# The last batch's tail beside the first shared steps, its first norm inside attention's first iteration, and the router in the second unit of each iteration

## The reference

```
h = layernorm(x) * (1 + ca) + sa
q, k = rms_norm(h) @ W + b;  v = h @ W_v + b          # 16 heads of 16
q, k = rotary(q), rotary(k)
weights = sigmoid(q k^T / 4);  weights /= sum(weights)
x = x + ga * ((weights @ v) @ W_o + b)
h = layernorm(x) * (1 + cb) + sb
shared = (silu(h @ sg) * (h @ su)) @ sd
probs = sigmoid(h @ router_w + routing_bias);  w = top-2 of 8, normalised
routed = sum_e w_e * (silu(h @ wg_e) * (h @ wu_e)) @ wd_e
x = x + gb * (shared + routed)
```

## Time and profile before

| | |
|---|---|
| median of 3 runs | 1613.15 us (1610.79 to 1613.45) |
| profiled execution | 1611.74 us, span 1610.0 us |
| PE busy | 1464.9 us (91%) |
| DVE busy | 1140.0 us (71%) |
| ACT busy | 929.5 us (58%) |
| POOL busy | 417.0 us (26%) |
| mean granted clock of PE | 0.953 |

### The profile page before, as it was taken

The page is one execution under the profiler, slowest core; times in us unless marked ns, Lnnn a source line. Parts: engine busy times, 40 slices in busy tenths (PEclk is TensorE's granted clock), DMA queues, the critical chain, the costliest instruction groups (busy, mean ns, idle before and its releaser), DMA issues. The chain is left out here.

```text
span 1610.0 us, 29263 instructions
## 1 busy us (share of the span) xinstructions
PE 1464.9 (91%) x10406; PEld 1172.9 (73%) x10406; DVE 1140.0 (71%) x2334; ACT 929.5 (58%) x1172; POOL 417.0 (26%) x413
## 2 busy tenths in 40 slices
PE   6899999868999977899999999866999999999998
PEld 4788888757888875355545544446889999999987
DVE  4677777568878875665786686455568787877768
ACT  2566665434555534776776676743347777777752
POOL 1122322330001012232153344223213333333320
PEclk9899999989999987999999999987999999999999
DMA  7000000210000000120000000005038888888864
GB/s 275 1 1 0 0 0 0 79 42 1 0 0 0 0 27 1 70 91 1 2 29 12 22 25 22 18 18 195 28 103 231 231 234 235 231 236 232 235 157 157
DMA packets 65455, 130.51 MB, mean 81 GB/s; under 512 B 8249, under 2 KB 38754, under 8 KB 64866
## 3 DMA queue, kind: packets, MB, share of 16 engines
q1 hardware_dynamic: 51074, 110.37, 22.1%
q0 software_dynamic: 14304, 19.15, 5.7%
HBM read 97.50 MB, written 32.00 MB: 80 GB/s over the span
## 5 line engine op out<-in xcount | busy, mean ns | idle before, releaser
L1822 ACT ACTIVATE at_wide<-at_sc_ps 128x2048 f32<-128x2048 f32 x128 | 240.6, 1879 | 117.3 <-PE at_sc_ps L1658 116.1
L2276 POOL DMA_INDIRECT sums<-e_y,e_row_ids x78 | 121.6, 1559 | 247.8 <-ACT e_y L2431 235.9
L52 PE MATMUL e_gate_ps<-e_h_parts,e_w 128*128 128x256 f32 (+1 forms) x1128 | 176.9, 304 | 7.0 <-DVE e_w L2485 3.4
L2485 DVE TENSOR_TENSOR e_w<-e_raw,e_w 128x1024 fp32r<-128x1024 f32 x123 | 147.1, 1222 | 42.7 <-ACT e_w L2384 42.7
L52 PE MATMUL e_up_ps<-e_h_parts,e_w 128*128 128x256 f32 (+1 forms) x1128 | 175.0, 302 | 0.0
L52 PEld LDWEIGHTS e_gate_ps<-e_h_parts,e_w 128*128 128x128 f32 x1128 | 155.3, 193 | 14.7 <-DVE e_w L2485 3.5
L52 PEld LDWEIGHTS e_up_ps<-e_h_parts,e_w 128*128 128x128 f32 x1128 | 155.2, 193 | 7.9
L1672 PE MATMUL at_o_ps<-at_wide,at_v_ones 128*32 128x512 f32 x1024 | 142.5, 630 | 0.0
L2341 PE MATMUL e_down_ps<-e_w,e_hidden 128*128 128x256 f32 x936 | 127.9, 286 | 1.0 <-DVE e_hidden L2534 1.0
L2384 ACT ACTIVATE e_w<-e_raw 128x1024 fp32r<-128x1024 f32 x123 | 125.3, 1048 | 6.1 <-DMA e_raw<-in_experts 6.1
L1658 PE MATMUL at_sc_ps<-at_qT,at_kT 32*128 32x512 f32 x1024 | 96.3, 450 | 28.9 <-ACT at_wide L1822 26.9
(11 more groups left out here) (351 smaller groups left out, 2735.2 us busy)
## 6 DMA issues: line engine op xcount, KB each, us to landing
e_raw<-in_experts SPq DMA_DIRECT2D x123, 512.0 KB
e_rows_in<-slots SPq DMA_DIRECT2D x39, 272.0 KB
sums<-shared SPq DMA_DIRECT2D x17, 256.0 KB
x<-in_L_attn_x SPq DMA_DIRECT2D x8, 512.0 KB, 9.4
gate<-gates SPq DMA_DIRECT2D x4, 1024.0 KB
slots<-shared SPq DMA_DIRECT2D x15, 272.0 KB
out<-x SPq DMA_DIRECT2D x7, 512.0 KB, 3.1
e_sums<-sums SPq DMA_DIRECT2D x4, 512.0 KB, 4.4
```

The costliest lines, as they stand in the source:

```text
L52: last = pe.matmul(out, left(i), right(j), start=n == 0, stop=n == len(steps) - 1)
L1822: nc.scalar.activation(wide[:, u % 2, :], sc_ps[:].rearrange("p n s -> p (n s)"), ACT.Sigmoid, scale=float(HD) ** -0.5).then_inc(sig_done, 1)
L2276: pool.indirect_dma_start(c.sums_dram[:, :], bass.IndirectOffsetOnAxis(ap=row_ids[:, j % 2, t:t + 1], axis=0), y[:, j % 2, t, :], None, co ...
L2485: nc.vector.tensor_tensor(w[:, buf, REST, q], raw[:, q], w[:, buf, HEAD, q].bitcast(F32), ALU.subtract).then_inc(w_split, 1)
```

## The change

The tail of batch 7 moves past the barrier. The weights of the shared expert are loaded while attention still runs, into a buffer `early` that also holds attention's `qk`, `turned` and `rotated`, once the last rotation is done. In the last part DVE adds the gated rows to x ahead of step 0, and takes statistics, places and normalises beside step 0; PE turns the batch behind step 0; ACT modulates it; router, first half of make_rows, probabilities and `choose` stand beside step 1, the token count behind it and the list of tiles beside step 2. Steps 0 and 1 are written out, with `beside` functions after product i. PE waits for each third of the weights apart.

The first norm of batch 7 moves from the head of attention into iteration 0 (statistics, norm, transposes in unit 14, modulation of half k=0 after sigmoid 15) and iteration 1 (half k=1 after sigmoid 0, the squares on PE after attend 0, their mean on DVE, the power on POOL). DVE keeps the first quarter of batch 0 before it rotates the last.

In iterations 2 to 7 rank and router move from unit 0 to unit 1, behind attend, into bank 1 of `a_ps`; the halves of make_rows go to the ends of units 0 and 3, values 2 and 3 from unit 1 to unit 2 (in all iterations), ACT's copies of rows to units 1 and 4 and its probabilities to unit 3. Waits follow the banks. On POOL the second cosine product and `bias_x` come earlier, two scatters a unit later.

```diff
+        self.early_loaded = [self.sem(f"early_loaded_{q}") for q in range(3)]
...
-        qk, turned, rotated = sb("qk", [P, 2, 2 * D]), sb("turned", [P, 2, 2 * D]), sb("rotated", [P, 2, 2 * D])
+        qk, turned, rotated = (c.early[:, n].rearrange("p (u n) -> p u n", u=2) for n in range(3))
...
+                sp.wait_ge(rot_done, NT * B)
+                for q in range(3):
+                    sp.dma_start(c.early[:, q], a["experts"][0][:, q]).then_inc(c.early_loaded[q], 16)
...
                     if coming:
                         times_cos(b + 1, 0)
+                        times_cos(b + 1, 1)
                     if b >= 3:
                         ds.tag(pool, b - 3)
                     scatter(b, 0)
-                    if coming:
-                        times_cos(b + 1, 1)
-                    scatter(b, 1, 5)
                     if past:
                         bias_x(b - 1)
+                    scatter(b, 1, 6)
                     scatter(b, 2, 7)
+                    if b == 1:
+                        pool.wait_ge(last_kept, 1)
+                        nc.gpsimd.tensor_tensor(c.inv_rms[:, B - 1], c.mean_square[:, B - 1], c.neg_half[:, 0:NT], ALU.pow
+                                                ).then_inc(last_kept, 1)
                     if past:
                         norm.invert(pool, b - 1)
-                    scatter(b, 3, 8)
+                    else:
+                        norm_last.invert(pool, 0)
+                    scatter(b, 3, 9)
                     scatter(b, 4, 10)
...
-                pool.wait_ge(last_kept, 1)
-                nc.gpsimd.tensor_tensor(c.inv_rms[:, B - 1], c.mean_square[:, B - 1], c.neg_half[:, 0:NT], ALU.pow
-                                        ).then_inc(last_kept, 1)
...
-                norm.invert(pool, B - 1)
...
+                        if b == 2 and t in (0, 2):
+                            pe.wait_ge(last_kept, 1)
                         if t == 0:
                             pe.wait_ge(h_split, b + 1)
                             if b >= 3:
-                                pe.wait_ge(logits_kept, b - 2)
-                            if b >= 4:
-                                pe.wait_ge(ds.placed, b - 3)
+                                pe.wait_ge(next_done, KC * (b - 3) + 1)
+                        if t == 2 and b >= 3:
+                            pe.wait_ge(logits_kept, b - 2)
                         if t == 2 and b >= 4:
-                            pe.wait_ge(ds.rows_kept, 2 * (b - 4) + 1)
+                            pe.wait_ge(ds.placed, b - 3)
...
+                    if b >= 2 and b < B - 1:
+                        pe.wait_ge(ds.rows_kept, 2 * (b - 1))
+                    if not coming:
+                        pe.wait_ge(logits_kept, b)
+                        pe.wait_ge(ds.placed, b - 1)
...
+                def last_by_feature():
+                    pe.wait_ge(qT_kept, NT * 2)
+                    pe.wait_ge(kT_kept, NT * 2)
+                    pe.wait_ge(last_rows_done, 1)
+                    transposes(nc.tensor, c, a_ps, rows_by_token(B - 1)).then_inc(last_turned, 1)
+
+                def sum_last_squares():
+                    pe.wait_ge(last_h_done, KC)
+                    pe.wait_ge(tables_set, 1)
+                    for t in range(NT):
+                        for k in range(KC):
+                            last = nc.tensor.matmul(a_ps[:, 1, t:t + 1], last_squares[:, k, t * P:(t + 1) * P], ones[:],
+                                                    start=k == 0, stop=k == KC - 1)
+                    last.then_inc(last_squares_done, 1)
...
-                        if u == 0 and b >= 2:
-                            pe.wait_ge(next_done, b - 1)
-                            if b >= 3:
-                                ds.rank(pe, b - 3, ranks)
-                            route(b - 2)
-                            if b >= 3:
-                                ds.make_rows(pe, b - 3, 0, a_ps[:, 1, :])
                         attend(b, par, u)
                         if u % NT == 1 and u > NT:
                             quad_by_token(b, u // NT - 1)
+                        if u == 14 and not past:
+                            last_by_feature()
+                        if u == 0 and b == 1:
+                            sum_last_squares()
...
+                                if b >= 3:
+                                    pe.wait_ge(ds.rows_kept, 2 * (b - 3) + 1)
+                                    ds.rank(pe, b - 3, ranks(1))
+                                if b >= 2:
+                                    route(b - 2, 1)
...
-                        if b >= 3 and u == 2:
-                            if coming:
-                                pe.wait_ge(v_kept, 2 * (b + 1) + 2)
-                            pe.wait_ge(ds.rows_kept, 2 * (b - 3) + 1)
-                            ds.make_rows(pe, b - 3, 1, a_ps[:, 1, :])
...
                                 values(b + 1, 0, 1)
-                            elif u == 1:
+                            elif u == 2:
                                 values(b + 1, 2, 3)
-                            elif u in (2, 3):
+                            if u in (2, 3):
...
+                        if b >= 3 and u == 0:
+                            pe.wait_ge(next_done, KC * (b - 1))
+                            ds.make_rows(pe, b - 3, 0, a_ps[:, 1, :])
+                        if b >= 3 and u == 3:
+                            if coming:
+                                pe.wait_ge(qk_scaled, NT * (b + 1) + 1)
+                            ds.make_rows(pe, b - 3, 1, a_ps[:, 0, :])
...
-                pe.wait_ge(last_rows_done, 1)
-                transposes(nc.tensor, c, o_ps, xn_last).then_inc(last_turned, 1)
...
-                ds.rank(pe, B - 2, sc_ps[:, 3, 0:NT * E])
-                next_by_feature(B - 1, False)
-                route(B - 1)
...
+                def modulate_last(k):
+                    act.wait_ge(last_turned, 1)
+                    shift, scale = c.mod[:, 1, SA, k, B - 1:B], c.mod[:, 1, CA, k, B - 1:B]
+                    nc.scalar.activation(c.hT[:, k, B - 1, :], a_ps[:, k, :], ACT.Identity, bias=shift, scale=scale)
+                    nc.scalar.activation(last_squares[:, k, :], a_ps[:, k, :], ACT.Square, bias=shift,
+                                         scale=scale).then_inc(last_h_done, 1)
...
+                        if u == 15 and not past:
+                            modulate_last(0)
+                        if u == 0 and b == 1:
+                            modulate_last(1)
...
-                        if b >= 3 and u in (1, 3):
-                            ds.keep_rows(act, b - 3, u // 2, a_ps[:, 1, :])
-                        if b >= 2 and u == 2:
+                        if b >= 3 and u == 1:
+                            ds.keep_rows(act, b - 3, 0, a_ps[:, 1, :])
+                        if b >= 3 and u == 4:
+                            ds.keep_rows(act, b - 3, 1, a_ps[:, 0, :])
+                        if b >= 2 and u == 3:
...
-                modulate(B - 1)
-                act.wait_ge(logits_kept, B)
-                ds.probabilities(act, B - 1)
...
                 def iteration(b, par, past, coming, h_after=True):
                     n, p = b + 1, b - 1
+                    if b == 1:
+                        dve.wait_ge(last_squares_done, 1)
+                        nc.vector.tensor_scalar(c.mean_square[:, B - 1], a_ps[:, 1, 0:NT], 1.0 / D, RMS_EPS, ALU.mult,
+                                                ALU.add).then_inc(last_kept, 1)
                     if past:
                         keep_quad(p, QUADS - 1)
-                    if b >= 2:
-                        keep_logits(b - 2)
-                    if b >= 3:
-                        ds.place_tokens(dve, b - 3, ranks)
                     if coming:
                         keep_values(n, 0)
                     if past:
                         divide_quad(p, QUADS - 1)
+                    if b >= 2:
+                        keep_logits(b - 2, 1)
+                    if b >= 3:
+                        ds.place_tokens(dve, b - 3, ranks(1))
...
+                        norm_last.gather(lambda t: c.x[:, B - 1, t, :])
+                        norm_last.aggregate(dve, 0)
...
+                        norm_last.apply(dve, 0, rows_by_token(B - 1), lambda t: c.x[:, B - 1, t, :], last_rows_done)
...
-                rotate(0, 3)
                 dve.wait_ge(strips_set, 2)
                 keep_by_feature(0, 0)
+                add_turned(0, 2)
+                rotate(0, 3)
...
-                update_x(B - 1)
-                moments(B - 1)
-                normalise(B - 1)
-                ds.place_tokens(dve, B - 2, sc_ps[:, 3, 0:NT * E])
-                keep_logits(B - 1)
...
+        raw = c.early
...
-                for q in range(PARTS):
-                    load_weights(0, q, a["experts"][0])
```

(93 more changed lines are left out.)

135 lines of the change are left out of this document (59 added, 76 removed).

## The result

The changed kernel takes 1591.87 us (median of 4 runs, 1589.79 to 1593.44) against 1611.97 for the kernel before (1609.64 to 1613.45): a ratio of 0.9878, with a 95% interval of 0.9864 to 0.9892, 20.1 us less. The prediction was 1595.3, with a range of 1589 to 1604. The profiled executions stand at 1593.44 and 1611.74, so the traces explain 18.3 us.

The account below looks back on a forecast made before the run. PE was taken to bound the shared and expert steps, and sigmoid, PE's extra work and clock falls attention's iterations. Terms -10.8 + 3.3 - 10.3 = -17.8 us against the profiled 1611.74, plus 1.4 to the median, gave 1595.3 us, range 1589 to 1604.

Parts of the forecast that it names:

- Part 1, the seam: Between attention and shared steps: 19.6 us gained, less 4.0 work, 4.0 waits and 0.8 clock, so -10.8 us.
- Work brought back, 4.0: Shared steps 0 to 2 on PE: rank 0.47, router 1.79, eight transposes 1.0, token count 0.7; together 4.0 us.
- The stall, 3.7: Step 1: PE waits 3.7 us before its last down products, behind table loads and choose; the tile list costs 0.3 in step 2.
- The clock behind the stall, 0.8: After step 1's stall: a clock fall would cost 1.6 us; half was taken, 0.8.
- rival 6: Step 1's two table switches also cost 1.38 us of drain each, 2.8 us more: 1598.1 us; chance 0.05.
- Part 2, the first norm: Attention's head and iterations 0 and 1: head -2.2 us, iteration costs and half a clock fall, net +3.3 us, a loss.
- Part 3, the router: Iterations 2 to 7: PE's work the same, gain from the clock no longer falling; two falls in six assumed, -10.3 us.
- 1 (all six fall): Iterations 2 to 7: the clock still falls briefly in all six, 6.4 us more: 1601.7 us; chance 0.17.
- 2 (no stall): Step 1: ACT and DVE reach the router's results earlier, so no stall, 3.7 + 0.8 less: 1590.8 us; chance 0.12.
- 3 (half of the gain given back at the tiles): Tiles: later scatters delay row loads and PE waits, losing 5.4 us, half the seam's gain: 1600.7 us; chance 0.08.
- 4 (the clock stays low behind the router): Iterations 2 to 7: long low-clock stretches, from about 8 us each, make the kernel slower; 1620 at 10.2 us; chance 0.04.
- 5: The change doesn't do what it says: early load lands no sooner, or another wait fills the seam; 1613; chance 0.04.

Follow-up runs that it names:

- e_seam_only: Kernel before with only attention's end cut off and the shared expert's weights loaded early; order and first norm as before: 1602.44 us, ratio 0.9955.
- e_router_only: Kernel before with only rank, router and first rows in their new places and values 2 and 3 in the third unit: 1602.25 us, ratio 0.9936.
- e_choose_later: Changed kernel with the last batch's choice on DVE moved behind step 1 and the tile list in two halves: 1585.13 us, ratio 0.9833.
- e_no_table: Changed kernel with the last batch's probabilities a copy of the logits, so ACT loads no table in step 1: 1589.19 us, one run.
- the second trace: The changed kernel, unedited, run again on the same chip as the two best versions: 1592.54 us, ratio 0.9877.
- e_norm_back: Changed kernel with the last batch's first norm back at attention's head, as in the kernel before: 1591.61 us, ratio 0.9878.
- e_squares_u1: Changed kernel with the last batch's sum of squares moved from the first to the second unit of iteration 1: 1588.60 us, ratio 0.9855.
- e_best_squares: Changed kernel with the squares in iteration 1's second unit and the last batch's choice behind step 1: 1582.20 us, ratio 0.9810.
- e_best_norm_back: Changed kernel with the first norm back at attention's head and the last batch's choice behind step 1: 1582.85 us, ratio 0.9811.
- e_router_twice: Changed kernel with the router's 16 products of each attention iteration done twice over, 32 in a row: 1617.39 us, one run.
- e_swap_attend: Kernel before with attend moved ahead of rank, router and rows in each iteration's first unit: 1611.15 us, ratio 0.9988.

## Why the prediction was right, point by point

The time was 3.4 us under the forecast, inside its own range of 1591 to 1599. Of these, 1.2 come from the kernel before, whose median is 1611.97 now and was 1613.15 in the forecast. Between traces -17.8 was forecast and -18.3 measured. The three parts miss by +1.2, +1.5 and -4.0, and attention began 0.9 later: the mechanisms were right, but that the sum came so close is in part luck. Three terms were off, all of them in part by the clock.

**Part 1, the seam: -10.8 forecast, -9.6 measured.**
- The first product 19.6 earlier: 18.9. It starts 4.6 us behind the end of the last gate product, forecast 4.7; the missing 0.7 lie ahead of that product (21.6 us from the last scores to its end, 20.9 before), and belong to part 3, as e_seam_only, which lacks them, and e_router_only, which has them, show.
- Work brought back, 4.0: 4.1, the 90.68 of e_choose_later less 86.59.
- The stall, 3.7, and 0.3 in step 2: 2.0 and nothing. The step that failed is ACT's count, in which the first table load stood behind the wait for the logits. In the trace it lies in front of it (1109.48, logits at 1110.53), and e_no_table shows what both loads cost, 0.95. Choose is 3.70 us from its start to the start of the rest behind it, where 4.04 was read to the end of its last instruction; start to start it was 3.96 there, so it is also 0.26 shorter here. 1.28 and 0.34 make 1.62 of the 1.7 missing. (The prediction calls the same stall 3.7 and 3.3 us; no term hangs on the second.)
- The clock behind the stall, 0.8 as half a fall: step 2 took 19.66 for 16.66, so 3.0 with the whole stretch of 6.8 us, and 0.5 more in the last down products and the counts ahead of step 2. Stall and clock together are 5.5 (96.23 less 90.68), forecast 4.8: the stall was put too high and the clock too low, and the two errors nearly cancel.
- The table rule of the Trainium skill, "ScalarE: Activation LUTs", What ACT_TABLE_LOAD costs, would have both switches cost their loads and 1.38 us of drain each. The trace agrees with the load (1.28) and has 0.02 us between its end and the next ACTIVATE; rival 6 is out.

**Part 2, the first norm: +3.3 forecast, +4.8 measured.** The head gave 2.66 (2.2; 2.0 and 1.8 in the second trace and in e_choose_later). Iteration 0 took 0.87 (1.24 in the second trace), where values and boundary had been put at 1.85. Iteration 1 was put at 2.85 without the clock, and is 53.92 where the clock holds: 51.07 + 2.85 (its first unit 5.49, forecast 5.4). With a clock fall of 10.2 us it took 57.66, with one of 3.4 us 54.76. The step that failed is the size of that fall: half of 1.6 where a whole one of 3.7 came in the first trace and one of 0.8 in the second.

**Part 3, the router: -10.3 forecast, -14.3 measured.** PE's units came out as summed (forecast 3.7, 4.35, 4.86, 3.7; iteration 4 has 3.76, 4.38, 4.67, 3.69). The term that was mis-sized is the number of falls: none of the two assumed, 3.2 of the 4.0; the other 0.8 is spread over all six iterations. Iteration 3 had a fall in e_router_only, e_norm_back, e_squares_u1 and e_best_squares and none in the two traces of the changed kernel, e_no_table, e_choose_later and e_best_norm_back; iteration 7 had one in e_choose_later. That the new place keeps the clock is shown: 12 falls in the 12 places of the two traces with the router in its old place (the kernel before and e_seam_only), five in 54 with it in the new one. The reason given, dense work on both sides and no wait, is argued: e_router_twice shows that the thin products count without a wait, e_swap_attend moved the wait instead of removing it, and no run has dense work on both sides together with a wait.

**Rivals.** 1 (all six fall): none did. 2 (no stall): it was there. 3 (half of the gain given back at the tiles): 0.42 us of idle time ahead of the first turned rows, waiting for the rows' load, and the last part 0.36 shorter, so no. 4 (the clock stays low behind the router): it does so with twice the products, never for more than 6.8 us. 5: each part did what it says.

What stays open is why one trace of the same iteration has the fall and another not. It is seen (iteration 1: 10.2, 3.4 and 0 us; iteration 3: 3.4 and 0), and it moves iteration 1 by up to 3.8 us. Executions of one kernel spread further: 7.0 us in e_router_only, 8.1 in e_best_norm_back, 11.0 in e_swap_attend, the fast ones at the higher mean clock. No run here controls it, and one trace a kernel doesn't price a fall that comes and goes.

## What to carry to other kernels

A group of thin products, such as a router, is worth trying behind dense products and away from a wait: moving 1.8 us of them by one unit returned 2.4 us an iteration (2.1 in e_router_only), without any work removed, and the values that had to give way cost 1.6 us once. A wait that a move creates is to be priced with the clock behind it: here a stall of 2.0 us cost 5.5 in the steps, and moving one 3.7 us step on another engine behind the operand that PE waits for got all of it back.

## What the runs showed of the hardware

- The granted clock fell to 0.50 (1.2 GHz) behind a stall of 2.00 to 2.02 us of PE in the shared steps in each of six traces, and not behind one of 1.05 us in the one trace that has it, with the same work around both.
- The length of the idle time alone does not decide: behind the turned rows PE stood 2.37, 2.19 and 2.19 us in three traces without a fall, and 2.21 us in the changed kernel's with one.
- It fell with PE fully busy: 32 products of 8 columns in a row, in a stretch of 20.01 us that PE filled entirely, gave a clock of 0.83 over that stretch; 16 in the same place gave 1.00 over 15.15 us.
- Identical code in iteration 1 got 10.2, 3.4 or 0 us at 0.50 in different executions. Run times go with the mean clock: 1577.81 us at 0.974 and 1585.86 at 0.968 for one and the same kernel (e_best_norm_back).
- An ACT_TABLE_LOAD ran before the semaphore wait of the activation that needed it (1109.48, while the logits came at 1110.53), so a switch of table ahead of a wait was free for as long as the wait lasted.
